# A vision block on one core: the first five token tiles embedded by full-precision products, with one norm chain for the first four

## The chip, the core and the metric

The kernel runs on one core of a Trainium2 chip. The core has TensorE (PE in the profile; it multiplies, from SBUF into PSUM), VectorE (DVE), ScalarE (ACT), GpSimd (POOL) and SyncE (SP), which here only issues transfers. Each engine works through its own list of instructions in order and waits at semaphores for the others. The metric is the device time of one execution in microseconds (us), the median of several runs; less is better.

## The reference, cut to what matters

```python
h = embed(x, W)                                  # 64 images, 14x14 patches of 768 values -> 256
z = layernorm(h)
mod = gelu(z @ mod_w1 + b1) @ mod_w2 + b2        # 256 -> 1024 -> 256
y = circular_convolution((z @ in_w + in_b) * mod, kernel)   # along the 196 tokens, by rfft
h = h + (y @ out_w + out_b)
h = h + ffn(layernorm(h))                        # dense base, shared low rank, 2 of 6 low-rank experts
```

All values are float32. There are 12544 tokens: 98 tiles of 128.

## The kernel before, in words

**Precision.** TensorE multiplies fp32r operands (rounded float32) in one pass. To keep float32 accuracy every operand is split in a rounded part, high, and the rest, low: ACT writes high, VectorE or GpSimd subtracts and writes low. `mm3` (L951 and on) then makes three products for one: high x high, low x high, high x low (L953 to L955). Operands of type float32 can be multiplied directly too; such a product shows as two instructions. The setup products (L1007, L1012), transposes and the inverse transform do this.

**Tiles and rounds.** Tokens are embedded in rounds (`intake_tiles`): round 0 has tiles 0 to 2, round 1 has tiles 3 and 4, each later round three. The contraction of 768 is cut in KT = 6 blocks of 128. The main loop has 32 steps, i = 1 to 32. Step i projects group mid = i - 1 (two images, 392 tokens), runs its MLP (eight `mlp_up` products, gelu on ACT, two `mlp_down`), embeds round i + 1, and does transforms and output for the groups i - 2 and i - 3.

**Ahead of step 1.** The order is written out by hand on every engine.
- SP loads the tokens of round 0 in three chunks (CHUNK = 2 blocks each), all of round 1 (`second_wait`), identity, bias, in_w, taps and w1; then `load_patches(2)` waits until the low parts of round 0 are done, and w2 and the rest stand behind it. ACT's queue issues the three chunks of the embedding weights.
- ACT rounds weights and tokens chunk by chunk (L513, L516), then round 1's tokens (L519), in_w and w1 (`split_hi`, L422). VectorE and GpSimd subtract (`first_rounds_lo`, L583 to L591 and L360, L364).
- TensorE (`first_rounds`) makes 54 products for round 0 into `rows_ps` and 36 for round 1 into `rotating`, then the two tap products (`spectrum_products`), `turn_x1(0)` (transposes of the normalised tiles), `shared_products` and `turn_x1(1)`.
- VectorE adds the output bias (`keep_h`), takes the statistics (`stats1`) and runs `layer_norm_scales`, 16 small steps one after the other (LN_STEPS, semaphore `dve_ln`), once for round 0 and once for round 1. ACT normalises each tile (`normalise`, L441), rounds the transposed tiles (`x1_hi`, L449), VectorE subtracts (`x1_lo`, L702).
- GpSimd waits for 2 x LN_STEPS before it splits w1 (L348). ACT rounds w2 and the tokens of round 2 (`patches_hi(2)`, L429); VectorE subtracts w2's parts (`split_w2`, L604) and signals `w2_lo`; GpSimd subtracts the tokens' (`patches_lo`, L354).

**Step 1.** TensorE's `project(0)` waits for both rounds' low parts and the splits of in_w and w1. Each `mlp_up(k)` waits for a gelu some tiles back; ACT's `gelu_tile(0, 0)` waits for `w2_lo`, as w2's last part is staged in the gelu buffer. After `mlp_up(7)` TensorE embeds round 2.

## Time and profile before

| | us |
|---|---|
| median of 3 runs | 1297.09 |
| lowest and highest | 1296.03, 1297.81 |
| the profiled execution | 1294.84 |
| its span | 1293.0 |

The profile follows one execution with a start and a length for every instruction. "Busy" is time in which an engine works; the bracket behind a row names the idle time ahead of it and whose result ended it. PEclk is TensorE's granted clock, 1.00 for 2.4 GHz and 0.50 for 1.2 GHz. The length of a matmul in the timeline takes in the way to PSUM; consecutive ones overlap, so their rate is read from the distance of their starts. The chain of waits gives each its share of the time. DMA times run from the issue to the last byte landed.

### The profile page before, as it was taken

The page shows a single profiled execution, that of the slowest core. Times are in us where ns is not written, and L with a number is a line of the kernel's source. Part 1 is how long each engine was busy: PE and PEld are TensorE (multiplying, and loading weights), DVE is VectorE, ACT ScalarE, POOL GpSimd, SP SyncE. Part 2 cuts the span into 40 slices and gives each one's busy share as a digit, 9 for nine tenths or more (in the row PEclk, how much of TensorE's full clock was granted, in tenths as well). Part 3 has the DMA queues.
Part 4 walks back from the last instruction along what each step waited for, and adds up shares of the span by engine and source line. Part 5 has one row for each costly group of instructions (what it writes and reads, how often), then busy time and mean ns, then how long its engine had stood idle before and what let it go on. Part 6 is the DMA issues. An engine that isn't in the chain of part 4 may idle for free.

```text
span 1293.0 us, 21070 instructions
## 1 busy us (share of the span) xinstructions
PE 1239.2 (96%) x8148; PEld 1199.4 (93%) x8148; DVE 868.5 (67%) x2584; ACT 585.6 (45%) x1108; POOL 399.8 (31%) x462
## 2 busy tenths in 40 slices
PE   5999999999999999999999999999999999999964
PEld 5999999999999999999999999999999999999953
DVE  6467666667766666766666776666677666677575
ACT  6644544444444445454444444443545444444410
POOL 4532333232233333233323223332323332322100
PEclk9999999999999999999999999999999999999986
DMA  7111111101111110111110111111011111010000
GB/s 236 37 38 50 49 50 38 49 13 50 49 50 50 37 39 24 50 49 50 37 50 13 50 49 50 50 37 46 18 50 49 50 37 50 15 48 13 13 1 33
DMA packets 23182, 57.18 MB, mean 44 GB/s; under 512 B 2665, under 2 KB 18218, under 8 KB 19114
## 3 DMA queue, kind: packets, MB, share of 16 engines
q1 hardware_dynamic: 22266, 55.05, 12.2%
q8 instruction: 64, 1.05, 0.4%
q10 hardware_dynamic: 816, 0.79, 0.2%
q14 instruction: 36, 0.29, 0.1%
HBM read 42.98 MB, written 12.85 MB: 43 GB/s over the span
## 4 chain that ended last, share of the span: by engine, by line
PE 90%; DVE 5%; ACT 2%; issue 1%; POOL 1%; DMA 0%; POOLq 0%; DVEq 0%
PE rotating L953 16%; PE rotating L955 16%; PE rotating L954 16%; PE rows_ps L953 10%; PE rows_ps L954 10%; PE rows_ps L955 10%; PE turn L1095 5%; PE turn L1079 2%; ACT x_h L449 2%; DVE x_l L702 2%; PE turn L992 2%; PE turn L953 1%; PE turn L954 1%; PE turn L955 1%; PE rotating L1060 1%
## 5 line engine op out<-in xcount | busy, mean ns | idle before, releaser
L471 ACT ACTIVATE gelu<-rotating,biases 128x392 f32<-128x392 f32 x256 | 149.0, 583 | 203.6 <-PE rotating L955 203.4
L382 POOL TENSOR_TENSOR folded<-modulated 128x196 f32<-128x196 f32 x64 | 38.5, 601 | 588.1 <-DVE modulated L793 588.1
L369 POOL TENSOR_TENSOR gelu_l<-gelu,gelu_h 128x784 fp32r<-128x784 f32 x62 | 117.1, 1889 | 225.8 <-DVE norm L776 199.8
L354 POOL TENSOR_TENSOR patches_l<-patches,patches_h 128x384 fp32r<-128x384 f32 x186 | 184.4, 1020 | 0.2 <-ACT patches_h L429 0.2
L953 PE MATMUL rotating<-gelu_h,w_h 128*128 128x392 f32 x512 | 177.6, 347 | 0.0
L953 PE MATMUL rotating<-x_h,w_h 128*128 128x392 f32 x512 | 177.1, 346 | 0.0
L953 PE MATMUL rows_ps<-tokw_h,patches_h 128*128 128x256 f32 x576 | 167.8, 291 | 7.5 <-POOL patches_l L360 7.5
L955 PE MATMUL rotating<-x_h,w_l 128*128 128x392 f32 x512 | 174.6, 341 | 0.0
L954 PE MATMUL rotating<-x_l,w_h 128*128 128x392 f32 x512 | 174.5, 341 | 0.0
L955 PE MATMUL rotating<-gelu_h,w_l 128*128 128x392 f32 x512 | 174.0, 340 | 0.0
L954 PE MATMUL rotating<-gelu_l,w_h 128*128 128x392 f32 x512 | 173.9, 340 | 0.0
L954 PE MATMUL rows_ps<-tokw_l,patches_h 128*128 128x256 f32 x576 | 162.0, 281 | 0.0
L955 PE MATMUL rows_ps<-tokw_h,patches_l 128*128 128x256 f32 x576 | 162.0, 281 | 0.0
L953 PEld LDWEIGHTS rows_ps<-tokw_h,patches_h 128*128 128x128 f32 x576 | 109.5, 190 | 16.1 <-DVE h_sb L864 8.7
L429 ACT ACTIVATE patches_h<-patches 128x384 fp32r<-128x384 f32 x186 | 80.4, 512 | 81.3 <-PE rows_ps L955 81.3
L476 ACT ACTIVATE gelu_h<-gelu 128x784 fp32r<-128x784 f32 x128 | 109.9, 859 | 3.0
L955 PEld LDWEIGHTS rows_ps<-tokw_h,patches_l 128*128 128x128 f32 x576 | 110.7, 192 | 0.0
L954 PEld LDWEIGHTS rows_ps<-tokw_l,patches_h 128*128 128x128 f32 x576 | 109.6, 190 | 0.0
L799 DVE TENSOR_TENSOR fold_l<-turn,fold_h 99x1024 fp32r<-99x1024 f32 x32 | 39.2, 1225 | 96.4 <-ACT fold_h L481 96.4
L441 ACT ACTIVATE norm<-rows_ps,ln_tmp 128x256 f32<-128x256 f32 x96 | 47.2, 560 | 120.6 <-DVE ln_tmp L688 120.6
L702 DVE TENSOR_TENSOR x_l<-turn,x_h 128x768 fp32r<-128x768 f32 (+23 forms) x48 | 32.3, 699 | 102.1 <-ACT x_h L449 102.1
L953 PEld LDWEIGHTS rotating<-x_h,w_h 128*128 128x128 f32 x512 | 96.1, 188 | 2.1
(203 smaller groups left out, 3007.2 us busy)
## 6 DMA issues: line engine op xcount, KB each, us to landing
patches<-dram_x_rest SPq DMA_DIRECT2D x31, 1152.0 KB, 5.1
out<-h_sb SPq DMA_DIRECT2D x32, 384.0 KB, 2.5
patches<-dram_x_first SPq DMA_DIRECT2D x3, 384.0 KB, 4.9
h_sb<-dram_x_second SPq DMA_DIRECT2D x1, 768.0 KB, 8.3
prod<-dram_tok_w ACTq DMA_DIRECT2D x2, 256.0 KB, 5.4
gelu<-dram_w SPq DMA_DIRECT2D x1, 512.0 KB, 6.4
norm<-dram_w SPq DMA_DIRECT2D x1, 384.0 KB, 6.1
gelu<-dram_w SPq DMA_DIRECT2D x1, 384.0 KB, 7.0
```

The lines of the kernel that those rows point to most:

```text
L354: pool.tensor_tensor(patches_l[:, k, :], patches[:, k, :], patches_h[:, k, :].bitcast(F32), ALU.subtract).then_inc(pool_patches_lo, 1)
L369: pool.tensor_tensor(gelu_l[:, 2 * j:2 * j + 2, :], gelu[:, 2 * j:2 * j + 2, :], gelu_h[:, 2 * j:2 * j + 2, :].bitcast(F32), ALU.subtract)\
L429: act.activation(patches_h[:, k, :], patches[:, k, :], ACT.Copy).then_inc(act_patches_hi, 1)
L441: ins = act.activation(norm1[:, t, :], ps, ACT.Identity, bias=ln_tmp[:, 1, which, t:t + 1], scale=ln_tmp[:, 0, which, t:t + 1])
L471: act.activation(gelu[:, k, :], bank(g + 1, UP[k])[:, 0:GT], ACT.Gelu, bias=b1_bias[:, k:k + 1]).then_inc(act_gelu, 1)
L476: act.activation(gelu_h[:, 2 * j:2 * j + 2, :], gelu[:, 2 * j:2 * j + 2, :], ACT.Copy)\
L702: ins = dve.tensor_tensor(x1_l[:, :, at:at + n], turn[:, :, off:off + n], x1_h[:, :, at:at + n].bitcast(F32), ALU.subtract)
L799: dve.tensor_tensor(fold_l[:, :, :], turn[0:NF, :, :], fold_h[:, :, :].bitcast(F32), ALU.subtract).then_inc(dve_fold_lo, 1)
L953: pe.matmul(ps, w_h, x_h, start=first, stop=False, skip_group_check=onto_read)
L954: pe.matmul(ps, w_h, x_l, start=False, stop=False, skip_group_check=onto_read)
L955: return pe.matmul(ps, w_l, x_h, start=False, stop=last, skip_group_check=onto_read)
L1095: ins = pe.matmul(inverted[:, m, img, x, 0:NFP], spec_y[0:NF, x, c:c + P], inverse[:, x, :], start=True, stop=True)
```

## The change

- `intake_tiles`: round 0 has tiles 0 to 3, round 1 only tile 4.
- The tokens of both rounds are loaded in four chunks of 1, 1, 2 and 2 blocks, tiles 0 to 2 and tiles 3 and 4 in turn, and the embedding weights in six loads of one block.
- TensorE embeds the five tiles by full-precision products of the loaded float32 values: 24 products for tiles 0 to 3 (tiles 0 to 2 into `rows_ps`, tile 3 into `rotating[:, 0]`), then 6 for tile 4 into `rotating[:, 1]`. No splits of their tokens are made. The embedding weights are still split for later rounds, low parts on GpSimd.
- One `layer_norm_scales` covers tiles 0 to 3. ACT normalises tiles 0 and 1, VectorE tiles 2 and 3 (`first_norms`). `keep_h(0)` comes after that and signals `first_h`, for which `shared_products` waits.
- ACT copies tile 4 from PSUM to SBUF (`fifth`). Its bias add, statistics and chain run on VectorE after `x1_lo(0)` and round 2's `patches_hi`, which is moved from ACT to VectorE. Its normalisation, transposes and splits are in step 1, after gelu 4 and `mlp_up(4)`, and after VectorE's second `gelu_lo`.
- `project(0)` needs only round 0's low parts and in_w; the first `mlp_up` waits for w1. `split_w2` follows the fifth tile's chain on VectorE. All of w2's first part is now staged in the gelu buffer too, so that `gelu_tile(0, 3)` waits for `w2_lo`, not `gelu_tile(0, 0)`.
- GpSimd's w1 split waits for LN_STEPS, not 2 x LN_STEPS. SP issues `load_patches(2)` after all constants, once tiles 0 to 3 are embedded.

```diff
-CHUNK = 2
+CHUNKS = ((0, 1), (1, 2), (2, 4), (4, 6))
...
-    return ((0, 1, 2), (3, 4))[r] if r < 2 else (3 * r - 1, 3 * r, 3 * r + 1)
+    return ((0, 1, 2, 3), (4,))[r] if r < 2 else (3 * r - 1, 3 * r, 3 * r + 1)
...
-            "w2": [(w2_v[:, 0:3, :], place(flat_norm2, 0, 3, DIM), w2_h[:, 0:3, :], w2_l[:, 0:3, :]),
+            "w2": [(w2_v[:, 0:3, :], place(flat_gelu, HID + DIM + DIM + 3 * DIM, 3, DIM), w2_h[:, 0:3, :], w2_l[:, 0:3, :]),
...
@@ sync @@
-                    sp.wait_ge(pool_first_lo, KT // 2)
-                    sp.wait_ge(dve_first_lo, KT // 2)
+                    sp.wait_ge(pe_embed, 2)
...
-            for n in range(KT // CHUNK):
-                ks = slice(n * CHUNK, (n + 1) * CHUNK)
-                sp.dma_start(patches[:, ks, :], x_first[:, ks, :]).then_inc(first_in[n], 16)
-            sp.dma_start(second_wait, x_second).then_inc(second_in, 16)
+            for n, (k0, k1) in enumerate(CHUNKS):
+                sp.dma_start(patches[:, k0:k1, :], x_first[:, k0:k1, :]).then_inc(first_in[n], 16)
+                sp.dma_start(second_wait[:, k0:k1, :], x_second[:, k0:k1, :]).then_inc(second_in[n], 16)
...
+            load_patches(2)
+            sp.wait_ge(tok_w_lo, KT)
+            sp.wait_ge(pe_embed, 4)
...
@@ gpsimd @@
-            first_rounds_lo()
+            tokw_lo()
             split_lo("in_w")
-            pool.wait_ge(dve_ln, 2 * LN_STEPS)
+            pool.wait_ge(dve_ln, LN_STEPS)
             split_lo("w1")
...
@@ scalar @@
-                if g == 0 and k == 0:
+                if g == 0 and k == 3:
                     act.wait_ge(w2_lo, 1)
...
             split_hi("in_w")
             split_hi("w1")
+            act.wait_ge(pe_embed, 4)
+            act.activation(fifth, rotating[:, 1, 0:DIM], ACT.Copy).then_inc(fifth_kept, 1)
             normalise(0, 0)
...
             x1_hi(0)
-            normalise(1, 1)
-            x1_hi(1)
             split_hi("w2")
-            patches_hi(2)
...
                 gelu_tile(mid, 4)
+                if i == 1:
+                    normalise(1, 1)
+                    x1_hi(1)
...
@@ vector @@
-            first_rounds_lo()
+            stats = stats1(0)
+            layer_norm_scales(0, stats, slice(0, 2), 2)
+            first_norms()
             keep_h(0)
-            stats = stats1(0)
-            layer_norm_scales(0, stats, slice(0, 1), 3)
+            x1_lo(0)
+            patches_hi(2)
             keep_h(1)
             stats = stats1(1)
-            layer_norm_scales(1, stats, slice(1, 2), 2)
-            x1_lo(0)
-            x1_lo(1)
+            layer_norm_scales(1, stats, slice(1, 2), 1)
             split_w2()
...
                     gelu_lo(mid, j)
+                    if i == 1 and j == 1:
+                        x1_lo(1)
...
@@ tensor @@
+            def first_block(ps, tiles, t, k):
+                return pe.matmul(ps[:, 0:DIM], tiles[:, k, t * TILE:(t + 1) * TILE], tokw_raw[k],
+                                 start=k == 0, stop=k == KT - 1)
+
             def first_rounds():
...
+                for n, (k0, k1) in enumerate(CHUNKS):
+                    pe.wait_ge(tok_w_in[n], 16 * (k1 - k0))
+                    pe.wait_ge(first_in[n], 16)
+                    for k in range(k0, k1):
+                        for t in range(3):
+                            first_block(rows_ps[:, t], patches, t, k)
+                        if k == k0:
+                            pe.wait_ge(second_in[n], 16)
+                        ins = first_block(rotating[:, 0], second_wait, 0, k)
                 ins.then_inc(pe_embed, 2)
                 for k in range(KT):
...
+                    ins = first_block(rotating[:, 1], second_wait, 1, k)
                 ins.then_inc(pe_embed, 2)
...
             def shared_products():
+                pe.wait_ge(first_h, 1)
...
-                pe.wait_ge(dve_x1_lo, g + 2)
+                pe.wait_ge(dve_x1_lo, g + 2 if g > 0 else 1)
...
             shared_products()
-            pe.wait_ge(dve_x1_lo, 1)
-            turn_x1(1)
...
                 if i == 1:
-                    pe.wait_ge(weight_lo, 2)
+                    pe.wait_ge(weight_lo, 1)
                     pe.wait_ge(spectrum_ready, 1)
                 project(mid)
...
+                if i == 1:
+                    pe.wait_ge(weight_lo, 2)
+                    pe.wait_ge(fifth_kept, 1)
                 mlp_up(mid, 0)
...
                 mlp_up(mid, 4)
+                if i == 1:
+                    turn_x1(1)
                 pe.wait_ge(act_gelu, HC * mid + 3)
```

## Rows read from the trace of the kernel before

**Rows 1.** Stretches: from:to, length, busy us (count) by engine, PEclk, DMA share, GB/s.
```profile
2.00:4.00 2.00, 0.00 (x0) 0.00 (x0) 0.00 (x0) 1.28 (x1) 0.00 (x0) 1.00 0.83 263
...
29.95:33.35 3.40, 3.40 (x10) 3.40 (x11) 3.40 (x3) 2.75 (x7) 3.23 (x3) 0.50 0.01 2
...
62.00:1230.00 1168.00, 1158.53 (x7685) 1124.42 (x7684) 795.93 (x2352) 541.47 (x1021) 365.19 (x419) 1.00 0.12 40
1230.00:1293.00 63.00, 32.65 (x170) 28.95 (x168) 40.02 (x151) 6.74 (x16) 2.51 (x6) 0.76 0.05 17
```

**Rows 2.** The chain of waits, first 30 us: start, length, what.
```profile
0.74 4.36 DMA prod<-dram_tok_w
...
12.71 0.21 PE rows_ps L955
...
14.90 0.11 PE rows_ps L955
...
25.09 4.81 POOL w_l L348 x3
29.95 0.69 PE rotating L953
```

**Rows 3.** TensorE's timeline: start, length, instruction, count, idle time before it.
```profile
7.47 0.55 PE L953 MATMUL rows_ps<-tokw_h,patches_h 128*128 128x256 f32 x1 [7.47 <-POOL patches_l L360]
...
16.09 0.28 PE L955 MATMUL rows_ps<-tokw_h,patches_l 128*128 128x256 f32 x1
...
20.57 1.10 PE L1007 MATMUL rotating<-gelu 64*99 64x256 f32 x4
22.60 0.88 PE L992 MATMUL turn<-ident,norm 128*128 128x128 f32 x6 [0.93 <-ACT norm L441]
...
42.26 0.28 PE L953 MATMUL rows_ps<-tokw_h,patches_h 128*128 128x256 f32 x1
```

**Rows 4.** The first line of the page.
```profile
span 1293.0 us, 21070 instructions
```

**Rows 5.** Token loads up to 45 us, issue to landing.
```profile
DMA to landing us min/median/max: 3.8/5.0/6.4
```

**Rows 6.** VectorE's timeline, same columns.
```profile
17.36 1.08 DVE L641 BATCH_NORM_STATS2 bn<-rows_ps 128x6 f32<-128x256 f32 x3
...
20.87 0.16 DVE L688 SCALAR_TENSOR_TENSOR ln_tmp<-mean_var,ln_tmp 128x3 f32<-128x3 f32 x1
...
29.67 1.04 DVE L604 TENSOR_TENSOR w_l<-norm,w_h 128x768 fp32r<-128x768 f32 x1 [1.29 <-ACT w_h L422]
30.63 1.50 DVE L604 TENSOR_TENSOR w_l<-spec_y,w_h 128x512 fp32r<-128x512 f32 x1
32.05 1.76 DVE L604 TENSOR_TENSOR w_l<-gelu,w_h 128x768 fp32r<-128x768 f32 x1
...
63.13 1.23 DVE L799 TENSOR_TENSOR fold_l<-turn,fold_h 99x1024 fp32r<-99x1024 f32 x1 [3.92 <-ACT fold_h L481]
```

**Rows 7.** ACT's timeline, same columns.
```profile
21.07 1.47 ACT L441 ACTIVATE norm<-rows_ps,ln_tmp 128x256 f32<-128x256 f32 x3 [3.61 <-DVE ln_tmp L688]
...
29.54 2.57 ACT L429 ACTIVATE patches_h<-patches 128x384 fp32r<-128x384 f32 x6
...
37.69 1.10 ACT L471 ACTIVATE gelu<-rotating,biases 128x392 f32<-128x392 f32 x2
...
62.07 1.03 ACT L481 ACTIVATE fold_h<-turn 99x1024 fp32r<-99x1024 f32 x1 [0.29 <-PE turn L1079]
```

**Rows 8.** GpSimd's timeline, same columns.
```profile
30.12 7.48 POOL L354 TENSOR_TENSOR patches_l<-patches,patches_h 128x384 fp32r<-128x384 f32 x6 [0.23 <-ACT patches_h L429]
```

**Rows 9.** A VectorE group, whole span: count, busy us, mean ns.
```profile
L694 DVE TENSOR_SCALAR norm<-h_sb,ln_tmp 128x256 f32<-128x256 f32 x98 | 34.6, 410 | 1.2
```

**Rows 10.** Two groups of TensorE products, whole span, same columns.
```profile
L953 PE MATMUL rows_ps<-tokw_h,patches_h 128*128 128x256 f32 x576 | 167.8, 291 | 7.5 <-POOL patches_l L360 7.5
...
L953 PE MATMUL rows_ps<-routedb_h,gated_h 97*128 97x256 f32 x96 | 28.0, 292 | 8.2 <-DVE gated_l L856 8.2
```

More of the change, by code:

```diff
@@ L186, in tower_program @@
         w2_lo = sem("w2_lo")
[L187 to L188 removed]
+        fifth_kept = sem("fifth_kept")
+        dve_first_norm = sem("dve_first_norm")
+        first_h = sem("first_h")
         setup_mm = sem("setup_mm")
@@ L428, in patches_hi @@
                 for k in range(KT):
[L429 removed]
+                    act.activation(patches_h[:, k, :], patches[:, k, :], ACT.Copy).then_inc(patches_hi_done, 1)
             def normalise(r, e):
                 act.wait_ge(dve_ln, LN_STEPS * (e + 1))
[L433 to L441 removed]
+                if r == 0:
+                    rows = [(norm1[:, t, :], rows_ps[:, t, 0:DIM], 0, t) for t in range(2)]
+                elif r == 1:
+                    rows = [(norm1[:, 0, :], fifth, 1, 0)]
+                else:
+                    rows = [(norm1[:, t, :], rows_flat[:, t * DIM:(t + 1) * DIM], 0, t) for t in range(TILES)]
+                for dst, src, which, t in rows:
+                    ins = act.activation(dst, src, ACT.Identity, bias=ln_tmp[:, 1, which, t:t + 1],
                                          scale=ln_tmp[:, 0, which, t:t + 1])
@@ L1241, with tiles_of @@
     x = x.reshape(IMAGES * N_TOK, KT, P)
-    def intake(r):
-        tiles = intake_tiles(r)
-        return x[tiles[0] * TILE:(tiles[-1] + 1) * TILE].transpose(2, 1, 0)
+    def tiles_of(first, last):
+        return x[first * TILE:(last + 1) * TILE].transpose(2, 1, 0)
     consts = shape_constants()
@@ L1251 @@
     arrays = {
-        "x_first": intake(0),
-        "x_second": intake(1),
-        "x_rest": np.stack([intake(r) for r in range(2, ROUNDS)]),
+        "x_first": tiles_of(0, 2),
+        "x_second": tiles_of(3, 4),
+        "x_rest": np.stack([tiles_of(intake_tiles(r)[0], intake_tiles(r)[-1]) for r in range(2, ROUNDS)]),
         "tok_w": a[pre + "tok_W"],
```

127 lines of the change are left out of this document (44 added, 83 removed).

## The prediction

> **What bounds the kernel now.** I read the stretches first [rows 1]. From 62 to 1230 us TensorE is busy 1158.53 of 1168 us. There the kernel is bound by its own products, and the change edits nothing in it. The last 63 us are not touched either. So all that can move is the time at which TensorE enters that dense part, and one microsecond there is one at the end. Next comes the chain of waits of the first 30 us [rows 2]: the load of the first weights until 5.1, later the split of w1 on GpSimd, 25.09 to 29.9, and behind it TensorE's first product of step 1 at 29.95. The timeline of TensorE [rows 3] gives the marks: first product 7.47, last of the first three tiles 16.1, two full-precision products at 20.57, transposes at 22.60, and embed of round 2 at 42.26. Between 29.95 and 42.26 it does not idle: 60 products. The mark to forecast is this 42.26, called E.
>
> The clock matters for E. A product of 256 columns takes 0.21 us of the chain up to 12.71 and 0.11 at 14.90, and the change comes at about 12.9 [rows 2]: 1.2 GHz from 7.47 on, for 5.4 us, then 2.4 GHz. (The clock column of the stretches has no record before its first change, so there the spacing shows it.) TensorE rests for most of 24.5 to 29.95, and from 29.95 to 33.35 the granted clock is 0.50 again [rows 1]: 3.4 us. So the two rows for a cold stretch after a restart are 3.4 and 5.4 us.
>
> The profiled execution took 1294.84 us (span 1293.0 [rows 4]), 2.25 below the median 1297.09 and below the lowest of the three. I make the sum on its marks and carry the difference over. Half of the 2 us between the two cold stretches is 1 us; a middle execution of the kernel before has a second cold stretch of about 4.4 us, and as products then run at half speed its E is 0.5 us later than 42.26.
>
> **The change part by part.**
>
> First products. They now wait for loads alone, not for ACT's rounding and the subtractions behind it. The first chunk is 128 KB of weights, 192 KB and 128 KB of tokens, 0.46 MB. By 4.0 us 0.53 MB have moved (2 us x 263 GB/s [rows 1]). The quickest load of 384 KB landed 3.8 us after its issue at 0.74, at 4.5 [rows 5]; the 256 KB of weights landed at 5.1 [rows 2]. With half the bytes in each I take 4.3, bounds 3.8 and 5.1. The other chunks are covered: even at 263 GB/s all 2.75 MB of these loads have moved by 4.0 + 2.2 / 0.263 = 12.4, and TensorE comes to the last chunk, its 17th product, at 13.9 by the next part.
>
> Their price. A full-precision product is two instructions; four took 20.57 to 21.67, which is 0.216 us apart plus the last one's end [rows 3]: 0.43 us a product at the fast clock, 0.86 at the slow one. A block of three rounded products costs 3 x 0.113 = 0.34 and 0.64. So each block costs more, but TensorE starts 3.2 us sooner. Four tiles are 24 products. With 5.4 us cold (the row of the same kind of start) the clock rises at 9.7; 6.3 products are done, 17.7 x 0.43 = 7.6 follow: 17.3. With 3.4 us cold it is 16.3. The row for this price has 64 contraction rows and not 128; rounded products of 97 and of 128 rows take 292 and 291 ns [rows 10], so I take it unchanged. The fifth tile (6 x 0.43) and the two tap products (0.86) end near 20.8, beside VectorE's chain: free.
>
> One norm chain. VectorE starts at 17.5: four statistics at 0.36 = 1.45 (three took 1.08, to 18.44), the small steps behind them to 21.03, 2.6 [rows 6]: 21.5. Before, the add of the bias (0.96) stood ahead of it and a second chain behind. ACT normalises two tiles, 1.0 of the 1.47 for three [rows 7], VectorE two beside it: 22.6. Eight transposes are 1.1 (six: 0.88 [rows 3]): 23.8. ACT rounds 128x1024, 1.03 as for the fold [rows 7]: 24.9. VectorE subtracts, 1.23 as for the fold [rows 6]: 26.2. GpSimd's w1 split starts at the end of the one chain, 21.5 + 4.8 = 26.3, and only the first mlp_up needs it. The shared product waits on TensorE for keep_h(0), which ends near 23.8, and is through by 25.6 even cold; no other queue is behind that wait. So project(0) starts at 26.2 and not 29.95: 3.75 us gained before step 1.
>
> What step 1 then pays. TensorE's own work up to mlp_up(4) is 42 products, 42 x 0.178 = 7.5, plus 2.2 for 4.4 us cold: ready at 35.9. But ACT's gelu of tile 3 now waits for w2_lo, and VectorE reaches the w2 split late. After 26.2 it has six token copies (moved from ACT, where six took 2.57 [rows 7]; I take 2.6), the fifth tile's bias add (0.7: between 0.4 alone and 0.96 beside GpSimd), its statistic (0.4), a whole chain (2.6): 32.5. Then the w2 splits, which took 1.04 + 1.50 + 1.76 beside GpSimd's token splits [rows 6, 8]. GpSimd's six (7.5 us [rows 8]) now run 26.6 to 34.1, so two are dear and the last is 1.04 like the first: w2_lo at 36.0. Bounds: 2.8 us for all three undisturbed (1.04 and two thirds of it), 4.3 for all disturbed, so 35.3 to 36.8.
>
> Then in ACT's queue: gelu 3, gelu 4 (0.53 each, two took 1.10 [rows 7]), the fifth tile's normalisation (0.55): 37.7. TensorE waits for that with mlp_up 5 to 7 queued behind: two transposes, 0.35, so mlp_up(5) at 38.0 and E at 38.0 + 3 x 1.07 = 41.2. Without any lateness of w2 the same queue would make it 35.9 + 0.2 + 0.55 + 0.55 + 0.4 = 37.6, E at 40.8: the new wait of TensorE for its own last gelu and a norm costs 1.7 us by itself, and w2 adds 0.4 on the rounded sum. GpSimd and SyncE: token splits end 34.1 where they ended 37.6, round 2's load is issued at 17.4 behind the other weights and lands by 23 (1.15 MB at 0.4 MB a us, plus 2), before VectorE wants it at 26.2. The weights behind SyncE's two waits go out near 20 as before. Free. After E nothing is new: gelu_hi(3) is 1.7 us behind E as before.
>
> Sum: E 41.2 against 42.26, 1.0 us gained on the profiled execution; against a middle one 1.5, as w2's chain covers the extra 0.5 us of cold clock. 1297.1 - 1.5 = 1295.6.
>
> At the six copies a rule speaks for less time. The nearest row is VectorE's scaling of 128x256 f32 from SBUF to SBUF, 0.410 us [rows 9]; with the 0.36 of a statistic of that width it is no faster a row than others. The Trainium skill, VectorE: DVE Perf Modes, section "The perf-mode tier table", gives copies and scalings of fp32 in SBUF the 2x mode; the row is a scaling and does not agree, and no row here shows a copy. By that rule the six would take some 1.6 us, an estimate from that page, and the forecast would be 0.4 us lower, since the other path then sets E.
>
> **The rivals.**
> (A) *The forecast*: E near 41, 1295.6.
> (B) *w2 drops off the path and the clock rises early.* After 3.4 us cold in the first stretch everything is 1.0 sooner, and a landing at 3.8 gives half of 0.5 more. If the copies are cheap as well, by a us, E is at 39.6 and the time 1297.1 - 0.5 - 2.7 = 1293.9. For it: the second cold stretch was 3.4 [rows 1]. Against: it takes two or three of these at once.
> (C) *VectorE and GpSimd hold each other up* (the side of slower). Of two VectorE subtractions of 128x768 the one wholly beside GpSimd's splits took 1.76 and the other 1.04 [rows 6]. If the copies pay that factor 1.7, they take 4.4, and the splits 4.3: w2_lo at 38.6, E at 43.9, the time 1297.1 - 0.5 + 1.6 = 1298.2. It decides from w2_lo at 37.4 on (no gain), and from 40 it is over 0.2% slower. The Trainium skill, GPSIMD Engine Reference, section "Key points", says that the two share their SBUF interfaces when VectorE uses a 2-port mode or two SBUF inputs; the disturbed subtractions agree. By it a copy in 2x mode would hold GpSimd, which has 2 us to spare.
> (D) *Full-precision products with 128 rows do not run at 0.43*, by unhidden weight loads or a clock that stays at 1.2 GHz. At 0.86 throughout the four tiles end at 4.3 + 20.6 = 24.9, 7.6 later: 1303.2. It turns slower than before once the 24 average 0.60 us; the forecast has 0.54. For it: only two products show the price; against: those two ran 0.216 an instruction with their weight loads beside them.
>
> **How the numbers follow.** A 0.55, B 0.28, C 0.10, D 0.07. About 0.2%, 2.6 us, is what a measurement of this kernel can tell from no change. The median of three also moves by about 1 us by itself (1296.03 to 1297.81; the end has a granted clock of 0.76 over 63 us [rows 1], untouched but not the same each time). A with that spread is 1294.0 to 1297.2 and gives 0.10 of its 0.55 to faster and none to slower. B gives 0.24 to faster, 0.04 to same. C gives 0.05 to same and 0.05 to slower, D 0.07 to slower. Faster 0.34, same 0.54, slower 0.12. The range takes in A, B to 1292.6 and C to 1298.4; D stands outside.
>
> **What would show it.** Right: TensorE's first product at 3.8 to 5.1, full-precision instructions 0.216 apart after the clock rises, the first chain ending near 21.5, project(0) near 26.2, TensorE idle 1.5 to 2.2 us ahead of the two transposes of the fifth tile, ACT's gelu 3 released by VectorE's w_l, and embed of round 2 near 41.2. Wrong: a granted clock of 0.50 beyond 11 us, an idle TensorE before 17 us, w_l ending after 37.4, or a dense part from 62 to 1230 us that is not as busy as before.

## The result, and the profile after

The median of the changed kernel is 1299.19 us (14 runs, 1296.06 to 1301.06), that of the kernel before beside it 1296.98 (14 runs): ratio 1.0019, 95% interval [1.0011, 1.0028]. It is 2.2 us slower. The forecast was 1295.6 and the range ended at 1298.4: wrong in direction, and outside.

The first line of the page, against [rows 4]. The execution took 1298.86 us.

```profile
span 1297.1 us, 20998 instructions
```

TensorE's timeline of the changed kernel (start, length, instruction, count, idle time before it and its releaser), against [rows 3]:

```profile
3.97 2.93 PE L953 MATMUL rows_ps<-prod,patches 128*128 128x256 f32 x6 [3.97 <-DMA prod<-dram_tok_w]
...
14.16 1.46 PE L953 MATMUL rows_ps<-spec_y,patches 128*128 128x256 f32 x6
15.46 0.59 PE L953 MATMUL rotating<-spec_y,h_sb 128*128 128x256 f32 x2
...
21.31 1.07 PE L986 MATMUL turn<-ident,norm 128*128 128x128 f32 x8 [1.63 <-ACT norm L435]
...
24.84 0.67 PE L943 MATMUL rotating<-x_h,inw_h 128*128 128x392 f32 x1 [1.08 <-DVE x_l L690]
...
34.95 0.34 PE L945 MATMUL rotating<-x_h,w_l 128*128 128x392 f32 x1
38.28 0.69 PE L986 MATMUL turn<-ident,norm 128*128 128x128 f32 x2 [2.99 <-ACT norm L435]
38.62 0.67 PE L943 MATMUL rotating<-x_h,w_h 128*128 128x392 f32 x1
...
43.03 0.28 PE L943 MATMUL rows_ps<-tokw_h,patches_h 128*128 128x256 f32 x1
```

Up to project(0) the change does what it says: 24.84 instead of 29.95, 5.1 us sooner. Then TensorE stands still for 2.99 us ahead of the two transposes of the fifth tile, and E, the start of the embed of round 2, is 43.03 instead of 42.26. Everything that was gained is given back, and 0.8 more.

The same stretch on VectorE, against [rows 6]:

```profile
23.47 1.23 DVE L690 TENSOR_TENSOR x_l<-turn,x_h 128x1024 fp32r<-128x1024 f32 x1 [0.89 <-ACT x_h L443]
24.61 5.22 DVE L572 CAST patches_h<-patches 128x384 fp32r<-128x384 f32 x6
29.75 1.22 DVE L603 TENSOR_TENSOR h_sb<-norm,out_bias 128x256 f32<-128x256 f32 x1
30.90 0.42 DVE L623 BATCH_NORM_STATS2 bn<-norm 128x6 f32<-128x256 f32 x1
...
33.95 0.16 DVE L676 SCALAR_TENSOR_TENSOR ln_tmp<-mean_var,ln_tmp 128x1 f32<-128x1 f32 x1
34.15 0.96 DVE L584 TENSOR_TENSOR w_l<-gelu,w_h 128x768 fp32r<-128x768 f32 x1
35.03 0.68 DVE L584 TENSOR_TENSOR w_l<-spec_y,w_h 128x512 fp32r<-128x512 f32 x1
35.63 0.95 DVE L584 TENSOR_TENSOR w_l<-gelu,w_h 128x768 fp32r<-128x768 f32 x1
```

GpSimd's and ACT's, against [rows 8] and [rows 7]:

```profile
25.33 6.52 POOL L353 TENSOR_TENSOR patches_l<-patches,patches_h 128x384 fp32r<-128x384 f32 x6 [0.30 <-DVE patches_h L572]
```

```profile
36.67 1.07 ACT L465 ACTIVATE gelu<-rotating,biases 128x392 f32<-128x392 f32 x2 [2.60 <-DVE w_l L584]
37.63 0.59 ACT L435 ACTIVATE norm<-norm,ln_tmp 128x256 f32<-128x256 f32 x1
```

These rows are one queue, read upward from TensorE's stall: the transposes wait for ACT's norm, the norm stands behind gelus 3 and 4, these wait 2.60 us for the last part of w2 (36.58), and that stands behind six copies, a bias add and a chain on VectorE. GpSimd is done at 31.85, where it ended at 37.60 [rows 8]; nobody wants that.

Stretches of the changed kernel (columns as in [rows 1]):

```profile
24.00:31.00 7.00, 6.16 (x19) 6.19 (x20) 7.00 (x9) 3.85 (x6) 6.70 (x7) 0.51 0.05 17
...
37.60:41.10 3.50, 2.82 (x10) 2.83 (x11) 1.46 (x3) 1.89 (x5) 0.00 (x0) 0.51 0.00 0
...
62.00:1200.00 1138.00, 1129.98 (x7511) 1096.93 (x7510) 775.22 (x2298) 529.27 (x1000) 361.60 (x415) 1.00 0.12 41
```

From 62 to 1200 us nothing has changed: the kernel before has TensorE busy 1129.97 us there. The granted clock is at 1.2 GHz twice in the front behind its first rise: around project(0), as before, and a second time from 37.7 to 41.1, behind the stall. Counting the start, that is a third cold stretch. It covers the products behind the transposes.

### The profile page after: what moved, and what is told of

Its sections match the earlier page's. It is cut to its first block, busy times and chain, and to the rows that moved or that the text cites. A ratio compares the mean times of both kernels' runs of the same rounds, so it can differ in the third digit from the quotient of the medians.

```text
span 1297.1 us, 20998 instructions
## 1 busy us (share of the span) xinstructions
PE 1246.4 (96%) x8118; PEld 1204.4 (93%) x8118; DVE 865.2 (67%) x2584; ACT 579.2 (45%) x1092; POOL 397.4 (31%) x462
## 4 chain that ended last, share of the span: by engine, by line
PE 90%; DVE 6%; ACT 3%; issue 1%; DMA 0%; POOL 0%; POOLq 0%; DVEq 0%; ACTq 0%
PE rotating L943 16%; PE rotating L945 15%; PE rotating L944 15%; PE rows_ps L943 10%; PE rows_ps L944 9%; PE rows_ps L945 9%; PE turn L1090 5%; PE turn L1074 2%; ACT x_h L443 2%; DVE x_l L690 2%; PE turn L986 2%; PE turn L943 1%; PE turn L944 1%; PE turn L945 1%; PE rotating L1055 1%
## 5 line engine op out<-in xcount | busy, mean ns | idle before, releaser
L943 PE MATMUL rows_ps<-tokw_h,patches_h 128*128 128x256 f32 x558 | 161.5, 289 | 0.0
L944 PE MATMUL rows_ps<-tokw_l,patches_h 128*128 128x256 f32 x558 | 156.0, 280 | 0.0
L945 PE MATMUL rows_ps<-tokw_h,patches_l 128*128 128x256 f32 x558 | 155.9, 279 | 0.0
L943 PEld LDWEIGHTS rows_ps<-tokw_h,patches_h 128*128 128x128 f32 x558 | 104.9, 188 | 8.6 <-DVE h_sb L852 8.6
L945 PEld LDWEIGHTS rows_ps<-tokw_h,patches_l 128*128 128x128 f32 x558 | 106.2, 190 | 0.0
L944 PEld LDWEIGHTS rows_ps<-tokw_l,patches_h 128*128 128x128 f32 x558 | 104.9, 188 | 0.0
L690 DVE TENSOR_TENSOR x_l<-turn,x_h 128x768 fp32r<-128x768 f32 (+24 forms) x48 | 32.3, 699 | 101.5 <-ACT x_h L443 101.5
```

Source lines behind the costliest of these rows:

```text
L690: ins = dve.tensor_tensor(x1_l[:, :, at:at + n], turn[:, :, off:off + n], x1_h[:, :, at:at + n].bitcast(F32), ALU.subtract)
L943: pe.matmul(ps, w_h, x_h, start=first, stop=False, skip_group_check=onto_read)
L944: pe.matmul(ps, w_h, x_l, start=False, stop=False, skip_group_check=onto_read)
L945: return pe.matmul(ps, w_l, x_h, start=False, stop=last, skip_group_check=onto_read)
```

## Experiments

Marks of all profiled executions. "w2 done" is the end of VectorE's last w_l, "turn" the first transpose of the fifth tile, "E" the embed of round 2, "project(31)" the first product of the last projection, "rest" the span's end less that. Ratios are to the kernel before, run beside each.

| kernel | project(0) | w2 done | turn | E | project(31) | rest | median us (runs) | ratio, 95% |
|---|---|---|---|---|---|---|---|---|
| before | 29.95 | 33.81 | | 42.26 | 1200.79 | 92.26 | 1296.98 (14) | |
| after | 24.84 | 36.58 | 38.28 | 43.03 | 1201.48 | 95.57 | 1299.19 (14) | 1.0019 [1.0011, 1.0028] |
| e13_after_again | 26.50 | 38.02 | 39.72 | 44.77 | 1202.55 | 93.95 | 1298.14 (11) | 1.0011 [1.0002, 1.0020] |
| e1_act_copies | 25.41 | 35.59 | 37.29 | 42.34 | 1200.57 | 94.00 | 1295.58 (10) | 0.9989 [0.9979, 1.0000] |
| e2_pool_waits | 25.41 | 36.74 | 38.44 | 43.49 | 1202.25 | 95.71 | 1299.78 (1) | |
| e3_turn_late | 26.64 | 38.12 | 43.77 | 43.91 | 1202.23 | 93.86 | 1297.98 (10) | 1.0012 [1.0001, 1.0022] |
| e4_fill_stall | 26.48 | 37.98 | 39.68 | 43.16 | 1201.67 | 94.03 | 1296.95 (10) | 1.0000 [0.9990, 1.0009] |
| e5_quiet | 26.55 | 33.67 | 36.95 | 41.20 | 1200.06 | 95.77 | 1297.47 (10) | 0.9995 [0.9985, 1.0006] |
| e6_quiet_turn | 26.63 | 33.83 | 39.14 | 42.13 | 1200.75 | 95.74 | 1298.26 (10) | 1.0000 [0.9988, 1.0012] |
| e8_all | 25.28 | 31.06 | 37.39 | 38.70 | 1197.29 | 93.94 | 1294.17 (7) | 0.9977 [0.9965, 0.9990] |
| e7_all_warm | 25.12 | 30.80 | 36.66 | 39.08 | 1197.62 | 95.93 | 1295.40 (11) | 0.9995 [0.9983, 1.0007] |
| e9_chain_quiet | 25.17 | 32.59 | 37.25 | 38.00 | 1196.17 | 94.28 | 1293.85 (9) | 0.9975 [0.9965, 0.9985] |
| e10_chain_warm | 26.66 | 33.97 | 38.16 | 40.12 | 1198.27 | 94.72 | 1292.92 (8) | 0.9970 [0.9960, 0.9980] |
| e11_before_warm | 29.37 | 33.24 | | 40.95 | 1199.05 | 94.20 | 1295.07 (10) | 0.9986 [0.9977, 0.9995] |
| e12_after_warm | 25.16 | 36.86 | 38.57 | 42.05 | 1200.19 | 93.87 | 1296.07 (10) | 0.9995 [0.9986, 1.0004] |
| e14_after_shift | 26.46 | 37.90 | 39.60 | 44.46 | 1204.27 | 94.12 | 1301.21 (5) | 1.0032 [1.0019, 1.0044] |
| e15_before_shift | 30.24 | 34.10 | | 42.73 | 1202.85 | 94.03 | 1297.10 (11) | 1.0005 [0.9996, 1.0014] |

Two things have to be known before single rows are compared. First, in the changed kernel and its variants project(0) comes at 24.8 to 25.4 in some traces and at 26.5 to 26.7 in others, also with the same code ahead of it ("after" and e13 are the same kernel). TensorE's clock decides it, at two places. It rose at 7.0 us in "after" and at 9.8 in e13, with the first product at 4.0 and 4.1, and e13's first transposes start 1.43 us later (22.74 against 21.31). In e13 it also fell again within these eight transposes, which took 1.30 us and not 1.07; the other late traces without fillers there (e3, e4, e5, e6, e14) have 1.26 to 1.90. So a trace is compared with the one of the two that has its project(0). Secondly, "rest" is code that no kernel here edits, and it took 92.3 to 95.9 us. The 92.26 of the profile of before is the shortest of all.

### The same kernel once more

No edit: e13_after_again is the changed kernel.

> Edit: none, the changed kernel once more, beside the kernel before. With the clock held in both (e11_before_warm 1295.07, e12_after_warm 1296.07) the changed kernel is 1.0 us slower, and 1.1 us later at the embed of round 2; unheld it was measured 2.2 us slower. Theory (the rest is chance of where the clock changes fall behind 1200 us, in code that is the same): the distance to before comes down to 0.8 to 1.8 us this time, and the profiled tail behind step 31 is another one than the 95.57 us of the first profile. Rival (the rest belongs to the changed kernel): 2.2 to 2.6 us again, and a tail of 95.6 us again.

It was 1.6 us above before (1298.14 against 1296.51), in the 0.8 to 1.8 of the theory, and its rest is 93.95 us, not 95.57. But its front is worse: E at 44.77.

```profile
22.74 1.30 PE L986 MATMUL turn<-ident,norm 128*128 128x128 f32 x8 [1.63 <-ACT norm L435]
...
26.50 0.66 PE L943 MATMUL rotating<-x_h,inw_h 128*128 128x392 f32 x1 [0.37 <-POOL w_l L347]
...
39.72 0.44 PE L986 MATMUL turn<-ident,norm 128*128 128x128 f32 x2 [3.79 <-ACT norm L435]
...
44.77 0.28 PE L943 MATMUL rows_ps<-tokw_h,patches_h 128*128 128x256 f32 x1
```

So the 3.3 us "behind 1200" in the first pair of traces are not all the changed kernel's own: its two executions differ by 1.6 us there. Two short stretches at the lower clock make up the 3.3 us (last section). The front costs between 0.8 (43.03 against 42.26) and 2.0 us (44.77 against the 42.73 of e15, which is the kernel before up to there).

### Who holds up VectorE

*The copies back on ACT.*

```diff
@@ scalar @@
             split_hi("w2")
+            patches_hi(2)
@@ vector @@
             x1_lo(0)
-            patches_hi(2)
             keep_h(1)
```

> The changed kernel with one thing undone: the six token copies of round 2 (patches_hi(2)) go back from VectorE to ACT, after the w2 rounding. Theory: what ate the 5 us gained ahead of step 1 is VectorE's queue in front of w2_lo (six copies of 0.87 us beside GpSimd), and then the clock that falls in TensorE's 3.0 us stall before the fifth tile's transposes. Then w2_lo comes near 33 instead of 36.6, gelu 3 waits for TensorE and not for w_l, the stall is 1.4 us or less, the clock stays at 2.4 GHz through it, and embed of round 2 starts near 39.8 instead of 43.0; the median is 2.5 to 3.5 us below the changed kernel's 1299.2. Rival (the loss sits at the end, behind 1200 us, and the front does not matter): embed of round 2 may move, the median stays near 1299.

The median came down by 3.6 us, to 1.0 below the kernel before, at the edge of its interval. That is what was expected, but by luck: the marks did not come, w2 done is 35.59 and not 33, E 42.34 and not 39.8. The two profiled executions are 2.5 us apart; 0.7 of it is E, and 1.6 the rest, which the edit does not touch. Five microseconds of copies left VectorE and w2 came 1.0 sooner. VectorE's timeline, and GpSimd's, say where they went:

```profile
25.18 0.70 DVE L599 TENSOR_TENSOR h_sb<-norm,out_bias 128x256 f32<-128x256 f32 x1
...
26.58 0.92 DVE L653 SCALAR_TENSOR_TENSOR ln_tmp<-ln_tmp 128x1 f32<-128x1 f32 x1
27.54 0.94 DVE L656 TENSOR_TENSOR ln_tmp<-ln_tmp 128x1 f32<-128x1 f32 x1
28.51 0.15 DVE L659 TENSOR_SCALAR ln_tmp<-ln_tmp 128x1 int32<-128x1 int32 x1
...
32.97 0.16 DVE L672 SCALAR_TENSOR_TENSOR ln_tmp<-mean_var,ln_tmp 128x1 f32<-128x1 f32 x1
```

```profile
26.48 5.86 POOL L353 TENSOR_TENSOR patches_l<-patches,patches_h 128x384 fp32r<-128x384 f32 x6 [0.88 <-ACT patches_h L424]
```

The chain works on a single element per partition. Steps with two operands in SBUF take 0.75 to 0.94 us while GpSimd subtracts tokens (26.48 to 32.34 in this trace), steps with one take 0.15, and as soon as GpSimd has ended all take 0.16. The chain lasts 6.9 us instead of 2.8. One of GpSimd's subtractions of 128x384 lasts 1.0 us (5.86 for six here). The six long steps end at 27.50, 28.48, 29.44, 30.41, 31.38 and 32.35, each 0.02 us behind the end of one of the six subtractions: each waits for it.

*GpSimd waits for all six copies.*

```diff
@@ gpsimd @@
             split_lo("w1")
+            pool.wait_ge(patches_hi_done, KT)
             patches_lo(2, range(KT))
```

> The changed kernel, but GpSimd starts its six low parts of round 2's tokens only when all six VectorE copies are done, so that the two do not run side by side. If the copies are slow because of GpSimd beside them, the six take 3.2 us or less instead of 5.1. If a rounding copy on VectorE simply costs 0.87 us, they still take 5.1 and w2_lo comes near 38 or later.

```profile
25.18 1.99 DVE L573 CAST patches_h<-patches 128x384 fp32r<-128x384 f32 x6
27.09 0.41 DVE L604 TENSOR_TENSOR h_sb<-norm,out_bias 128x256 f32<-128x256 f32 x1
```

This is one execution, and only its trace is read. With GpSimd's token parts held back, the same six copies take 1.99 us and not 5.22, and the bias add 0.41 and not 1.22. The contention is shown. A copy costs 0.33 us here, where the first is still beside GpSimd's w1 split (until 25.60), and 0.28 in e5 below, where none is. Nothing is gained, since the chain now runs beside GpSimd and takes from 27.87 to 34.3: w2 done 36.74 where it was 36.58.

*GpSimd waits for w2.*

```diff
@@ gpsimd @@
             split_lo("w1")
+            pool.wait_ge(w2_lo, 1)
             patches_lo(2, range(KT))
```

> The changed kernel with one wait more: GpSimd starts round 2's low parts of the tokens only when VectorE has signalled w2_lo. Everything from VectorE's six copies to the last w2 subtraction then runs without GpSimd beside it. Theory (VectorE and GpSimd shut each other out for whole instructions): copies 2.0 us, bias add 0.4, chain 2.7, subtractions 2.5, so w2_lo near 32.7 and not 36.6 (for a project(0) at 24.8); gelu 3 is released by TensorE; the stall ahead of the fifth tile's transposes is 1.4 us, the clock holds, and embed of round 2 starts near 40. GpSimd ends its token parts near 38.6, in time. Median 2.5 to 3.5 us below the changed kernel's. Rival (the copies alone were the cost, as when they went back to ACT): w2_lo is no earlier than the 35.6 of that run.

Copies (1.69 us for six), bias add, chain and splits all run alone, and w2 is done at 33.67, 4.3 us before e13's 38.02 with the same project(0). E is 3.6 us sooner, 41.20. The bound has changed hands, though: TensorE's 0.58 us ahead of E are now a wait for GpSimd, which ends at 41.06.

```profile
26.33 1.69 DVE L573 CAST patches_h<-patches 128x384 fp32r<-128x384 f32 x6
```

```profile
33.75 7.31 POOL L353 TENSOR_TENSOR patches_l<-patches,patches_h 128x384 fp32r<-128x384 f32 x6 [7.45 <-DVE w_l L585]
```

The median, 1297.47, shows less of it than the trace: 0.7 us below e13, 1.7 below "after", where 2.5 to 3.5 were expected. Part of that is in the profile: behind E this execution lost 1.1 us up to project(31) and 1.8 in the rest (95.77) against e13's. Part is in how executions spread. Three of e5's ten took 1294.2 to 1295.5 us and seven 1297.2 to 1297.8; of e6's ten three took 1293.6 to 1294.0 and seven 1297.9 to 1299.3. With such groups a median tells mostly in which of them more executions fell. Both profiles are of the upper group.

### Whose wait the stall is, and what the clock adds

*The fifth tile later.* Its norm goes behind gelu_hi(1) on ACT, its transposes behind mlp_up(7), and its roundings and subtractions behind the last gelu's.

```diff
@@ scalar @@
                 gelu_tile(mid, 4)
-                if i == 1:
-                    normalise(1, 1)
-                    x1_hi(1)
                 gelu_hi(mid, 1)
+                if i == 1:
+                    normalise(1, 1)
...
                 gelu_hi(mid, 3)
                 if i == 1:
+                    x1_hi(1)
@@ vector @@
-                    if i == 1 and j == 1:
+                    if i == 1 and j == 3:
                         x1_lo(1)
@@ tensor @@
                 mlp_up(mid, 4)
-                if i == 1:
-                    turn_x1(1)
...
                 mlp_up(mid, 7)
+                if i == 1:
+                    turn_x1(1)
```

> The changed kernel with the fifth tile's normalisation, transposes and splits moved behind: the normalisation after gelu_hi 1, the transposes after mlp_up 7, its low part after the last gelu_lo. TensorE then no longer waits for its own last gelu plus a norm. gelu 3 is still released by w2_lo at 36.6, so mlp_up 5 starts near 37.3 instead of 38.6 after an idle time of about 2.2 us. Theory: embed of round 2 starts at 40.7 if the clock holds through 2.2 us, at 42 if it falls as it did in the 3.0 us stall. Rival (end only): the median stays near 1299.

The stall stays (3.22 us), as a wait for ACT's gelu, whose own wait for w2 has not changed (38.12), and the clock falls behind it as before. E is 0.9 us sooner than e13's (43.91). The fifth tile's norm and transposes are thus 0.9 us of the loss. The median moved by 0.2 us against e13, which is inside its error.

*The stall filled*, with 14 products whose results nobody reads.

```diff
@@ tensor @@
                 mlp_up(mid, 4)
                 if i == 1:
+                    for _ in range(14):
+                        pe.matmul(turn[:, 0, 0:GT], w1_h[:, 0, 0:P], x1_h[:, 0, 0:GT], start=True, stop=True)
                     turn_x1(1)
```

> The changed kernel plus 14 products of 392 columns whose result nobody reads (2.5 us of TensorE work), put between mlp_up 4 and the fifth tile's transposes, where TensorE idles 3.0 us. Theory: nothing else moves, but the clock stays at 2.4 GHz, so the six to eight products behind the stall cost 0.18 and not 0.33 us and embed of round 2 starts 1.2 us earlier, near 41.8. Rival: the clock falls for another reason than the idle time, and embed starts near 43 again.

```profile
35.39 2.66 PE L1144 MATMUL turn<-x_h,w_h 128*128 128x392 f32 x14
39.68 0.44 PE L986 MATMUL turn<-ident,norm 128*128 128x128 f32 x2 [1.63 <-ACT norm L435]
```

The turn comes where e13 has it, but the clock stays at 2.4 GHz and E follows after 3.48 us, where e13 needs 5.05 and "after" 4.75. The third cold stretch costs 1.3 to 1.6 us. The median is 1296.95, 1.2 below e13's, and no longer to be told from before.

*Both clocks held.* The two kernels are compared with fillers in all their idle times.

```diff
@@ tensor, e12_after_warm @@
             spectrum_products()
+            pe.wait_ge(tok_w_hi, KT)
+            for _ in range(12):
+                pe.matmul(turn[:, 0, 0:DIM], tokw_h[:, 0, 0:P], tokw_h[:, 0, :], start=True, stop=True)
             turn_x1(0)
             shared_products()
+            for _ in range(10):
+                pe.matmul(rows_ps[:, 1, 0:DIM], tokw_h[:, 0, 0:P], tokw_h[:, 0, :], start=True, stop=True)
...
                 if i == 1:
+                    for _ in range(28):
+                        pe.matmul(turn[:, 0, 0:GT], w1_h[:, 0, 0:P], x1_h[:, 0, 0:GT], start=True, stop=True)
                     turn_x1(1)
```

e11_before_warm has 8, 15 and 24 products of 256 columns in the kernel before: ahead of turn_x1(0), ahead of turn_x1(1) and behind it.

> Edit: the kernel before with 8, 15 and 24 products of 256 columns, whose results nobody reads, in TensorE's idle stretches of the front. The clock is taken out of the comparison. Both theories: clock 2.4 GHz from its first rise until step 1 is under way, project(0) at 29.9 as before, embed of round 2 at 40.6, which is 42.26 less half of the 3.35 us that the trace of before has at the lower clock. Theory (the queue behind w2_lo is most of the change's loss): with e12_after_warm at 41.8, the changed kernel is still about 1.2 us later at this mark although it starts project(0) 5 us sooner. Rival (the clock is most of it): the two kernels come within 0.3 us or the changed one comes out ahead.

> Edit: the changed kernel with 12 and 10 products of 256 columns in the idle stretches ahead of project(0) and 28 of 392 columns in the stall ahead of the fifth tile's turn, none of them read. Theory (queue): project(0) at 24.9, w2_lo at 36.6 and the turn at 38.3 as in the changed kernel, embed of round 2 at 41.8 since the products behind the turn run at the higher clock; a median 1.5 to 2 us below the changed kernel's, and the embed 1.2 us later than e11_before_warm's. Rival (clock): embed at 40.6 or sooner. Where the fillers lengthen the stall, the turn comes behind 38.6.

Timelines of TensorE, of e11:

```profile
29.37 0.45 PE L953 MATMUL rotating<-x_h,inw_h 128*128 128x392 f32 x1 [0.22 <-POOL w_l L348]
...
40.95 0.28 PE L953 MATMUL rows_ps<-tokw_h,patches_h 128*128 128x256 f32 x1
```

and of e12:

```profile
32.63 5.18 PE L1149 MATMUL turn<-x_h,w_h 128*128 128x392 f32 x28
38.57 0.44 PE L986 MATMUL turn<-ident,norm 128*128 128x128 f32 x2 [0.76 <-ACT norm L435]
...
42.05 0.28 PE L943 MATMUL rows_ps<-tokw_h,patches_h 128*128 128x256 f32 x1
```

In both the clock stays at 2.4 GHz from its first rise until behind E. E is 42.05 against 40.95, 1.10 us later, and the medians are 1296.07 and 1295.07, 1.00 apart. This is the queue behind w2 by itself: about 1 us of loss for a kernel that starts step 1 4.2 us sooner. Holding the clock gave the kernel before 0.7 us between project(0) and E (11.58 against 12.31), and the changed one 1.3 to 1.6 between turn and E (3.48). So the clock takes 0.5 to 0.8 us more from the changed kernel. With the queue's 1.1 that makes 1.6 to 1.9 us at E; the medians differ by 1.6 and 2.2. The rival, that the clock is most of the loss, falls, though a third or more of it is the clock's. One limit stays: the two traces are single ones, both with an early first rise (10.1 us in e11, where before has 12.9). No run holds the clock behind a late rise; unheld, the marks of e13 and e15 are 2.0 apart.

### Everything together

*e6_quiet_turn* is e5's edit with e3's, *e8_all* is e6's with e1's, and *e7_all_warm* is e8's with e12's 12 and 10 products.

> The wait of the run before (GpSimd after w2_lo) and, besides, the fifth tile's transposes after mlp_up 7. With w2_lo early, the only stall left in step 1 was the fifth tile's own: the theory expects TensorE to run from project(0) through mlp_up 7 without an idle time over 0.5 us, and embed of round 2 near 38.7, where GpSimd's token parts end; median 1 us below the run before. Rival (the 1.4 us stall is hidden by something that ends later anyway): no difference to the run before.

> As the run before, and the six copies on ACT. VectorE's w2_lo then comes near 30.6, GpSimd's token parts end near 36.6, and ACT is late by some 1 us with the first x_proj and gelu. Embed of round 2 is then bound by TensorE alone, near 38.0 with the second cold stretch in front; the median is at or just below that of the run before (0 to 1 us).

> As the run before, plus 22 products of 256 columns whose result nobody reads, 12 between the tap products and the first transposes and 10 after the shared products, where TensorE is idle. Theory (the second cold stretch is caused by these idle times and costs half its length): the clock stays at 2.4 GHz from its first rise on, project(0) takes 0.18 us a product, and embed of round 2 starts near 36.7; median 1.5 to 2.5 us below the run before, so near 1292. Rival (the clock falls all the same, or the fillers delay the transposes): no gain, or up to 0.5 us lost.

```profile
42.13 0.36 PE L944 MATMUL rows_ps<-tokw_h,patches_h 128*128 128x256 f32 x1 [2.61 <-POOL patches_l L353]
```

In e6 TensorE has its products done sooner and then waits 2.61 us for GpSimd, whose six parts take 8.08 us beside more of VectorE's gelu subtractions (7.31 in e5): E is 42.13, later than e5's, where 38.7 was expected. There is no gain. e8 frees VectorE of the copies, so that GpSimd can start at 31.14: E 38.70, and the median 1294.17 is below before, interval [0.9965, 0.9990]. In e7 the clock stays up and TensorE just waits longer for GpSimd (2.04 us): E 39.08. Its median is 1.2 us above e8's and not to be told from before. The filler products buy nothing while GpSimd ends last.

*e9_chain_quiet* is e8 with the wait that the kernel before had; *e10_chain_warm* adds the 12 and 10 products.

```diff
@@ gpsimd, against e8_all @@
             split_lo("w1")
-            pool.wait_ge(w2_lo, 1)
+            pool.wait_ge(dve_ln, 2 * LN_STEPS)
             patches_lo(2, range(KT))
```

> Edit: the kernel of e8_all (the third copy of patches_hi on ScalarE, the fifth tile's turn handled late, GpSimd's patches_lo held back), but GpSimd waits only for the end of the fifth tile's norm chain, 2*LN_STEPS on dve_ln, as the kernel before does, and no longer for w2_lo. Theory (the chain is what needs GpSimd silent, the w2 splits do not): the chain ends as in e8 near 28.6, GpSimd starts there, three w2 splits beside it take up to 4 us in place of 2.4, w2_lo near 33, still ahead of the gelu that needs it; GpSimd's six parts end near 36, so TensorE sets the embed of round 2 at 37.5 to 38 in place of 38.7; median at or a little below that of e8, 1293 to 1294, below both kernels. Rival (the w2 splits need GpSimd silent too): w2_lo behind 34, the gelu of TensorE's third product late, embed at 38.7 or later and a median at or above e8's 1294.2.

> Edit: e9_chain_quiet with 12 and 10 products of 256 columns, whose results nobody reads, in TensorE's two idle stretches ahead of project(0). Theory (the clock's fall at project(0) is on the path): the granted clock stays 2.4 GHz from 7 us through the front, project(0) at 25 as before, embed of round 2 at 36.8 to 37.3, 0.5 to 1.5 us below e9. Rival (GpSimd's parts end behind the products, as in e7): embed at 38 or later, a wait of TensorE on patches_lo, and no gain over e9.

VectorE, GpSimd and TensorE of e9:

```profile
28.33 0.16 DVE L673 SCALAR_TENSOR_TENSOR ln_tmp<-mean_var,ln_tmp 128x1 f32<-128x1 f32 x1
28.52 0.96 DVE L581 TENSOR_TENSOR w_l<-gelu,w_h 128x768 fp32r<-128x768 f32 x1
29.40 1.50 DVE L581 TENSOR_TENSOR w_l<-spec_y,w_h 128x512 fp32r<-128x512 f32 x1
30.82 1.77 DVE L581 TENSOR_TENSOR w_l<-gelu,w_h 128x768 fp32r<-128x768 f32 x1
```

```profile
28.57 9.29 POOL L353 TENSOR_TENSOR patches_l<-patches,patches_h 128x384 fp32r<-128x384 f32 x6 [3.20 <-DVE ln_tmp L673]
```

```profile
38.00 0.36 PE L939 MATMUL rows_ps<-tokw_h,patches_h 128*128 128x256 f32 x1 [0.38 <-POOL patches_l L353]
```

The chain is undisturbed (2.4 us from 26.02), the three w2 splits share the time with GpSimd, 4.1 us, and w2 is done at 32.59: in time. E is 38.00. GpSimd ended at 37.86 and not near 36, as its six parts pay too: 9.29 us. The median is 1293.85, 3.0 us below before, 5.3 below the changed kernel's and 4.3 below e13's; it is in the 1293 to 1294 of the theory. Against e8's 1294.17 it is no measured difference. e10's E is 40.12, far from the 36.8 to 37.3 expected: this execution had its clock rise late (9.9) and project(0) at 26.66, and TensorE then waited 1.57 us for GpSimd. That was the longest of its eight executions. Its median, 1292.92, is 0.9 below e9's, with intervals that overlap by most of their width. Both beat both kernels.

### Is the rest of the distance chance?

The same 16 products of 256 columns are put into step 3 of either kernel.

```diff
                     pe.wait_ge(dve_h, i)
+                    if i == 3:
+                        for _ in range(16):
+                            pe.matmul(turn[:, 0, 0:DIM], tokw_h[:, 0, 0:P], tokw_h[:, 0, :], start=True, stop=True)
                     turn_x1(i + 1)
```

> Edit: the changed kernel with 16 products of 256 columns, whose results nobody reads, in step 3 ahead of the turn of x1; at the higher clock they take 1.7 us, and everything behind comes that much later. Theory (the clock changes behind 1200 us fall by chance from run to run): the median is 1.7 us above that of e13_after_again, give or take 0.7. Rival (their place is fixed against the kernel's own start, so that a kernel has a tail of its own): the tail changes from 95.6 toward 94 with the shift and the median moves by less than 0.7 us, or by more than 2.7.

> Edit: the kernel before with the same 16 products in the same place of step 3. Theory (chance): 1.7 us above the kernel before, 1298.4 give or take 0.7. Rival (a tail of the kernel's own): the tail behind step 31, 92.26 us in the profile of before, changes toward 95 with the shift, and the median moves by more than 2.7 us; then the difference of the two kernels is partly one of phase, and the shifted kernels stand otherwise to one another than the unshifted ones.

In the traces the delay is what it should be: project(31) less E is 1159.8 in e14 and 1160.1 in e15, where it is 1157.8 in e13 and 1158.5 in before. The medians do not follow evenly. The changed kernel went up by 3.1 us (1301.21, five runs only, against 1298.14), the kernel before by 0.6 (1297.10 against 1296.51). Neither is 1.7 give or take 0.7, so the theory "chance from run to run" is not confirmed. Both lie where e14's rival put a median, under 0.7 or over 2.7; e15's rival, over 2.7, did not come. Against the rival speaks that the rest in e14, 94.12 us, is that of the unshifted e13. In the kernel before it went from 92.26 to 94.03, and there is no second unshifted profile to tell whether the shift did that. So it stays open whether a kernel has a tail of its own. What stands is this: a pure delay of 1.7 us moves a median of some ten runs by anything from 0.6 to 3.1, and differences of 1 us between two kernels here must not be read from medians alone. The 1.0 us of e11 and e12 rests on their marks E, 1.10 apart, and the medians only agree.

## Why the prediction was wrong

Point by point, in the order of its own steps. Where two numbers stand, the first is the first profile, the second e13.

- **First products and their price**: right. First product 3.97 (4.3 forecast), full-precision instructions 1.30 us for six, 0.216 apart, so rival D is gone. The clock rose at 7.0 and at 9.8; the prediction had taken 9.7 and kept the other for B.
- **One norm chain**: right, and project(0) with it: 24.84 and 26.50, forecast 26.2 for a late rise and 1.0 less for an early one. The two are 1.7 apart and not 1.0: 1.4 because the rises are 2.8 us apart and not 2, 0.2 because in e13 the clock fell again within the first transposes.
- **VectorE's stretch from the end of x1_lo(0) to w2**: the step that failed. 9.8 us were forecast; it took 11.9 and 11.7. Of its terms the copies were 2.6 and measured 5.2 and 5.0, the bias add 0.7 against 1.2, the w2 splits 3.5 against 2.4, as GpSimd was done by then. Statistic and chain were 3.0 against 3.2. The failure is not the duration of a copy: alone it is 0.28 us (e5), even less than the 0.43 forecast. It is that each operation was priced alone, or by a factor, where the two engines exclude one another for whole instructions: the last four of the six copies, wholly beside GpSimd's parts, start 1.08 us apart, one to each part.
- **ACT's queue behind w2**: right, 1.70 us from w2 to the turn in both traces.
- **TensorE behind the turn**: 3.5 us forecast, 4.75 and 5.05 measured. The forecast had the clock fall only once more behind its rise, at project(0) (4.4 us cold there). The stall that it named itself, 1.7 us, grew to 3.0 and 3.8, and the clock fell a third time behind it. Held, it is 3.48 (e4, e12). The cold stretch at project(0) had 6.0 and 3.7 us of its length behind project(0); the stall hides that.
- **Sum**: for e13, 0.2 (front) + 1.9 (VectorE) + 1.5 (clock) = 3.6, and 44.77 is 3.6 above 41.2. For the first profile, -1.5 + 2.1 + 1.25 = 1.85, and 43.03 is 1.8 above.
- **Behind E nothing is new**: right. From E to project(31) it is 1158.5 us before and after, 1158.6 in e8; the lowest is 1157.8 (e13), the highest of the unshifted 1158.9 (e5).
- **Rival C** named the mechanism and gave E 43.9 and 1298.2. The two traces lie on either side of it, in part by luck: its w2 at 38.6 is later than both (36.6 and 38.0), and it has no third cold stretch. Without that stretch its border was too late as well: it had the gain end with a w2 at 37.4, and in the first profile a w2 at 36.58 left none. It got a chance of 0.10, too little: the rows of before had one disturbed subtraction, 1.76 us against 1.04 [rows 6], and the change puts VectorE's whole path beside GpSimd's six parts. In the kernel before this is avoided by one wait, 2 x LN_STEPS on GpSimd; the change halves it, and the prediction read that as a gain for w1 and looked no further at what then runs beside the second chain.
- **The rule on copies** (the Trainium skill, VectorE: DVE Perf Modes, "The perf-mode tier table": fp32 copies in SBUF have the 2x mode) was set aside for a row of scalings. e2 and e5 bear the rule out for copies: 0.28 us for 128x384 alone, against 0.41 for a scaling of 128x256 [rows 9]. Six took 1.69 in e5, where the estimate by that page was 1.6.
- **The rule on the shared interfaces**: the prediction said by it that a copy would hold GpSimd. The trace shows both held, and VectorE far more: 1.08 us from copy to copy and not 0.28, while GpSimd's part took 1.09 and not 1.0. The Trainium skill says so too, on another page than the one weighed: SBUF — State Buffer, "SBUF: two separate sides", has the pair of ports locked for a whole instruction, by whichever starts first, when VectorE's operation has two SBUF inputs or a 2-port mode. The steps of 0.92 (two inputs) and 0.15 (one) in e1 agree with it.

So 1.6 to 1.9 us of loss are accounted for: 1.1 by the queue behind w2, 0.5 to 0.8 by the third cold stretch, beyond what the clock costs the kernel before. Open is how the places of the clock's changes depend on a kernel; "rest" differs by up to 3.7 us in the table.

## What to carry to other kernels

Before work is moved on VectorE or GpSimd, list what the other one runs in the same microseconds, and price every VectorE operation that has two SBUF inputs, or is a copy like the ones here, with up to the length of one GpSimd instruction on top, however small it is. A chain of tiny steps is the worst thing to put there: in e9 GpSimd is silent for 3.2 us while the chain runs. With the copies on ACT and the fifth tile late as well, 4.3 of the 4.8 us won ahead of step 1 reach E there, and 3.0 the median. A stall that a change opens on TensorE costs its own length and then the clock behind it: here 3.0 to 3.8 us of stall brought 1.3 to 1.6 more.
